# A graph-attention layer on one core: attention scores in two groups of three units over three banks, with other engine orders and the last two batches written out

## What is computed

```
h = relu(layernorm(x))                       # x: (32, 256, 384)
q, k, v = h @ Wq + bq, h @ Wk + bk, h @ Wv + bv
scores = einsum('bhqd,bhkd->bhqk', q, k) / 8
probs  = softmax(scores + where(adj, 0, -9e15))   # adj: (32, 256, 256)
ctx    = einsum('bhqk,bhkd->bhqd', probs, v)
out    = x + ctx @ Wf + bf
```

## Time and profile before

| what | value |
|---|---|
| time, median of 3 runs | 593.15 us (592.7 to 593.23) |
| the profiled execution, its own time | 594.17 us |
| its span, first to last instruction | 592.4 us |
| PE, PEld busy | 575.3 us, 429.6 us |
| ACT, POOL, DVE busy | 516.3 us, 491.4 us, 473.5 us |
| mean granted PE clock | 0.994 of full speed |

### The profile page before, as it was taken

One profiled execution on the slowest core, in us unless ns is written; L12 is line 12 of the kernel. 1 busy time (PEld: TensorE's weight loads), 2 busy tenths in 40 slices (PEclk: granted clock), 3 DMA queues, 4 the chain that ended last, 5 costly groups with the idle time before them and its releaser, 6 DMA issues.

```text
span 592.4 us, 17738 instructions
## 1 busy us (share of the span) xinstructions
PE 575.3 (97%) x6640; PEld 429.6 (73%) x6640; DVE 473.5 (80%) x1484; ACT 516.3 (87%) x1161; POOL 491.4 (83%) x533
## 2 busy tenths in 40 slices
PE   7997999999999999999999999999999999999986
PEld 7676777777777777777777777776777777777754
DVE  5988888888878878888887888888787778878664
ACT  2788999899999999999999999998999999999972
POOL 2779998888899888889988888988888898888870
PEclk9999999999999999999999999999999999999999
DMA  8048889879788989879897977789897787978662
GB/s 273 8 77 148 134 169 177 170 159 168 165 148 157 185 157 178 167 141 168 160 184 157 181 163 150 159 158 177 165 178 166 157 151 161 179 132 153 125 133 73
DMA packets 275640, 92.01 MB, mean 155 GB/s; under 512 B 257633, under 2 KB 275554, under 8 KB 275554
## 3 DMA queue, kind: packets, MB, share of 16 engines
q1 hardware_dynamic: 274352, 90.87, 79.8%
q10 hardware_dynamic: 1202, 0.01, 0.1%
HBM read 17.05 MB, written 12.58 MB: 50 GB/s over the span
## 4 chain that ended last, share of the span: by engine, by line
PE 82%; DVE 6%; ACT 5%; DMA 3%; issue 2%; POOL 1%; ACTq 0%; SPq 0%; DVEq 0%; POOLq 0%
PE ring L1043 18%; PE ring L1045 18%; PE ring L1044 18%; PE scores L1106 11%; PE ctx L1129 5%; PE ring L1141 3%; PE ctx L1131 3%; PE ctx L1130 3%; DMA p_cols<-p_rows 2%; DVE logits L750 2%; ACT probs L550 2%; DVE h_rows L767 1%; DMA bf_row<-in_L_gnn_bf_dram 1%; ACT qk L575 1%; PE ring L1171 1%
## 5 line engine op out<-in xcount | busy, mean ns | idle before, releaser
L428 POOL TENSOR_TENSOR p_rows<-probs,p_rows 128x512 f16<-128x512 f32 x190 | 220.6, 1161 | 32.2 <-ACT p_rows L555 31.8
L750 DVE CUSTOM_DVE_ANT_0 logits<-scores,mask,logit_unscale 128x256 f32<-128x256 f32 x384 | 169.0, 478 | 61.6 <-PE scores L1106 61.4
L550 ACT ACTIVATE probs<-logits,raised 128x256 f32<-128x256 f32 x372 | 168.9, 501 | 6.0
L1043 PE MATMUL ring<-h_cols,w_hi 128*128 128x256 f16 x576 | 157.2, 273 | 0.0
L1045 PE MATMUL ring<-h_cols,w_lo 128*128 128x256 f16 x576 | 157.0, 273 | 0.0
L1044 PE MATMUL ring<-h_cols,w_hi 128*128 128x256 f16 x576 | 156.9, 272 | 0.0
L414 POOL TENSOR_TENSOR split<-qk,split 128x512 f16<-128x512 f32 x96 | 111.5, 1161 | 36.4 <-DVE split L774 36.4
L555 ACT ACTIVATE p_rows<-probs 128x512 f16<-128x512 f32 x190 | 119.7, 630 | 6.0
L575 ACT ACTIVATE qk<-ring,qk_bias_s,qkv_ratio 128x256 f32<-128x256 f32 x192 | 96.5, 552 | 3.7 <-PE ring L1045 3.7
L1129 PEld LDWEIGHTS ctx<-v_hi,p_cols 128*128 128x128 f16 x756 | 68.9, 97 | 33.2 <-issue 27.7
L1129 PE MATMUL ctx<-v_hi,p_cols 128*128 128x65 f16 x756 | 88.2, 195 | 4.1 <-DMA p_cols<-p_rows 2.0
(11 more groups left out here) (116 smaller groups left out, 1158.6 us busy)
## 6 DMA issues: line engine op xcount, KB each, us to landing
x_in<-in_x_dram SPq DMA_DIRECT2D x32, 384.0 KB, 3.9
out_dram<-result SPq DMA_DIRECT2D x62, 192.0 KB, 2.2
p_cols<-p_rows SPq DMA_TRANSPOSE x190, 3.2
adj_in<-in_adj_dram SPq DMA_DIRECT2D x32, 64.0 KB, 2.9
w_raw<-in_L_gnn_Wq_dram SPq DMA_DIRECT2D x1, 576.0 KB, 5.6
w_raw<-in_L_gnn_Wv_dram SPq DMA_DIRECT2D x1, 576.0 KB, 8.0
w_raw<-in_L_gnn_Wf_dram SPq DMA_DIRECT2D x1, 576.0 KB, 9.0
h_cols<-h_rows SPq DMA_TRANSPOSE x29, 4.7
```

Of the source, the lines that this page charges most:

```text
L428: pool.tensor_tensor(p_rows[u][:, 1], probs[u % 3][:], p_rows[u][:, 0], ALU.subtract).then_inc(p_lo_ready, 1)
L550: act.activation(probs[u % 3][:, a], logits[u % 3][:, a], ACT.Exp, bias=raised[u % 3][:, a:a + 1], scale=-1.0).then_inc(probs_ready, 1)
L750: dve.tensor_tensor_reduce(out=logits[u % 3][:, a], in0=score_bank[a][:, u % 2 * S:(u % 2 + 1) * S], in1=mask[b.parity][:, t], scale=logit ...
L1043: pe.matmul(out_ap, a_hi, m_hi, start=first, stop=False)
```

## The change

It has four parts.

- **Three banks, groups of three.** The bank that held the start's peaks becomes a third score bank. `scores(b, units)` takes any units, and in a cycle it is called with units 0 to 2 and 3 to 5, 18 matmuls each. `score_of` places the six blocks. A block of unit 0's head 0 and one of unit 2's head 1 share a bank, and so PE waits, before the first matmul of the latter, for the last of the former (`shared_bank_done`).
- **Other orders in a cycle**, on DVE, POOL, ACT and SP.
- **The last two batches** (`PREV`, batch 30, and `LAST`, batch 31) are written out on each engine instead of the last call of `cycle` and the end; `cycle` runs for b = 1 to 29. A few buffers change banks there.
- **The start**: batch 0 is scored as (0, 1), (2), (3), (4, 5).

```diff
@@ constants and banks @@
-    GROUPS = UNITS // 2
+    GROUPS = UNITS // C
-        score_bank = [bank("scores0"), bank("scores1")]
-        peak_bank = bank("peaks")
+        score_bank = [bank(f"scores{n}") for n in range(3)]
+        peak_bank = score_bank[2]
+        def score_of(u, a):
+            n, column = ((1, 0), (2, 0), (0, 0), (2, S), (0, S), (1, S))[u % C * 2 + a]
+            return score_bank[n][:, column:column + S]
-            for k in range(1, B - 1):
+            for k in range(1, B - 2):
@@ scores on PE @@
-            def scores(b, g):
-                for u in (2 * g, 2 * g + 1):
+            def scores(b, units):
+                for u in units:
                     if u < C:
                         wait(pe, qk_hi_ready, b.count(C, u + 1))
                         wait(pe, qk_lo_ready, b.count(C, u + 1))
-                wait(pe, logits_ready, b.count(2 * UNITS, 4 * g))
-                for u in (2 * g, 2 * g + 1):
+                wait(pe, logits_ready, b.count(2 * UNITS, 2 * units[0]))
+                for u in units:
                     t, tile = u // C, split[b.parity][u % C]
                     for n, (q, k) in enumerate(((1, 2), (1, 3), (0, 2))):
                         for a in range(2):
+                            if u % C == 2 and n == 0 and a == 1:
+                                wait(pe, shared_bank_done, b.count(GROUPS, u // C + 1))
                             own = slice(D * a, D * a + D)
-                            mm = pe.matmul(score_bank[a][:, u % 2 * S:(u % 2 + 1) * S],
-                                           tile[own, q, t * P:(t + 1) * P], tile[own, k],
+                            mm = pe.matmul(score_of(u, a), tile[own, q, t * P:(t + 1) * P], tile[own, k],
                                            start=(n == 0), stop=(n == 2))
+                            if u % C == 0 and n == 2 and a == 0:
+                                mm.then_inc(shared_bank_done, 1)
                 mm.then_inc(scores_ready, 1)
@@ PE, cycle @@
-                    if here and u % 2 == 0:
-                        scores(b, u // 2)
+                    if here and u % C == 0:
+                        scores(b, range(u, u + C))
@@ POOL, cycle: the third split ahead of add_bias @@
                 if here:
                     probs_lo(b, 3)
                 if front:
+                    split_lo(b + 1, 2)
+                if here:
+                    probs_lo(b, 4)
+                if front:
                     add_bias(b + 1)
-                if here:
-                    probs_lo(b, 4)
-                if front:
-                    split_lo(b + 1, 2)
@@ DVE, cycle: unit 2 read ahead of v_lo; rows split behind unit 3; third cast behind the moments @@
                 if here:
+                    mask_and_max(b, 2)
                     v_lo_part(b, 0)
                     v_lo_part(b, 1)
-                if here:
-                    mask_and_max(b, 2)
+                if (b + 3).exists():
+                    layer_stats(b + 3, (0,))
                 if front:
                     qk_hi_part(b + 1, 0)
                 if before:
                     context_lo(b + -1, 0)
-                if (b + 2).exists():
-                    h_lo_rows(b + 2)
                 if here:
                     mask_and_max(b, 3)
                 if before:
                     divide(b + -1, 1)
+                if (b + 2).exists():
+                    h_lo_rows(b + 2)
                 if front:
                     qk_hi_part(b + 1, 1)
...
                 if here:
                     mask_and_max(b, 4)
-                if front:
-                    qk_hi_part(b + 1, 2)
                 if (b + 3).exists():
                     layer_stats(b + 3, (1,))
                     layer_moments(b + 3)
+                if front:
+                    qk_hi_part(b + 1, 2)
@@ PE, the end, up to the last probabilities @@
-            scores(LAST, 0)
+            scores(PREV, (0, 1, 2))
+            apply_probs(PREV + -1, 2)
+            project_qk(LAST, 0)
+            project_out(PREV + -2, 1)
+            scores(PREV, (3, 4, 5))
+            apply_probs(PREV + -1, 3)
+            transpose_context(PREV + -1, 0)
+            project_qk(LAST, 1)
+            apply_probs(PREV + -1, 4)
+            apply_probs(PREV + -1, 5)
+            project_qk(LAST, 2)
+            project_v(LAST, 0, (0,))
+            transpose_context(PREV + -1, 1)
+            project_v(LAST, 0, (1, 2))
+            project_out(PREV + -1, 0)
+            apply_probs(PREV, 0)
+            scores(LAST, (0, 1, 2))
+            project_v(LAST, 1)
+            apply_probs(PREV, 1)
             apply_probs(PREV, 2)
             project_out(PREV + -1, 1)
+            scores(LAST, (3, 4, 5))
             apply_probs(PREV, 3)
-            scores(LAST, 1)
             transpose_context(PREV, 0)
             apply_probs(PREV, 4)
-            scores(LAST, 2)
+            project_out(PREV, 0)
             apply_probs(PREV, 5)
-            project_out(PREV, 0)
```

More of the change, by code:

```diff
@@ L261, in pair, with scored @@
             return slice(j * P, (j + 1) * P)
+        def scored(b, u):
+            if b.k == 0:
+                return (1, 1, 2, 3, 4, 4)[u]
+            return 4 + (b.k - 1) * GROUPS + u // C + 1
         def w_scale(n):
@@ L517, in cycle @@
                 if front:
-                    split_lo(b + 1, 2)
+                    add_bias(b + 1)
             cycles(cycle)
@@ L524, in raise_last @@
                 pool.wait_ge(logits_ready, LAST.count(2 * UNITS, 2 * u + 2))
-                pool.tensor_scalar(raised[u % 3][:], least[u % 3][:], P_RAISE, None, ALU.add).then_inc(raised_ready, 1)
+                pool.tensor_scalar(raised[u % 3][:], least[u % 3][:], P_RAISE, None, ALU.add)\
+                    .then_inc(raised_last_ready, 1)
+            probs_lo(PREV + -1, 5)
+            add_bias(LAST)
+            split_lo(LAST, 0)
+            probs_lo(PREV, 0)
+            probs_lo(PREV, 1)
+            probs_lo(PREV, 2)
+            make_mask(LAST)
+            split_lo(LAST, 1)
+            split_lo(LAST, 2)
+            probs_lo(PREV, 3)
+            probs_lo(PREV, 4)
+            raise_last(0)
             probs_lo(PREV, 5)
-            raise_last(0)
             raise_last(1)
@@ L707, in context_hi_last @@
                 act.activation(ct_hi[1][:, chunks].rearrange("p c q -> p (c q)"),
-                               R_CT[1][:, chunks.start * P:chunks.stop * P], ACT.Copy).then_inc(ct_hi_ready, 1)
+                               ct_of(LAST, 1)[:, chunks.start * P:chunks.stop * P], ACT.Copy).then_inc(ct_hi_ready, 1)
+            v_hi_part(PREV, 1)
+            exps(PREV, 0)
+            qk_full(LAST, 0)
+            probs_hi(PREV, 0)
+            exps(PREV, 1)
+            exps(PREV, 2)
+            probs_hi(PREV, 1)
+            context_hi(PREV + -1, 0)
+            qk_full(LAST, 1)
+            probs_hi(PREV, 2)
+            exps(PREV, 3)
+            probs_hi(PREV, 3)
+            qk_full(LAST, 2)
+            exps(PREV, 4)
+            probs_hi(PREV, 4)
+            exps(PREV, 5)
+            v_hi_part(LAST, 0)
+            context_hi(PREV + -1, 1)
+            probs_hi(PREV, 5)
             exps_last(0)
+            v_hi_part(LAST, 1)
             probs_hi(LAST, 0)
-            v_hi_part(LAST, 1)
             exps_last(1)
@@ L715, in _ @@
             exps_last(2)
+            context_hi(PREV, 0)
             probs_hi(LAST, 2)
-            context_hi(PREV, 0)
             exps_last(3)
@@ L721, in _ @@
             exps_last(5)
+            context_hi(PREV, 1)
             turned_hi(4, 1)
-            context_hi(PREV, 1)
             turned_hi(5, 2)
@@ L742, in mask_and_max @@
                 t, j = u // C, u % C
-                wait(dve, scores_ready, b.count(GROUPS, u // 2 + 1))
+                wait(dve, scores_ready, scored(b, u))
                 if u == 0:
@@ L1010, in finish_last @@
                                          op1=ALU.add).then_inc(result_ready, 1)
+            mask_and_max(PREV, 0)
+            divide(PREV + -1, 0)
+            mask_and_max(PREV, 1)
+            mask_and_max(PREV, 2)
+            qk_hi_part(LAST, 0)
+            finish(PREV + -2, 1)
+            v_lo_part(PREV, 0)
+            mask_and_max(PREV, 3)
+            mask_and_max(PREV, 4)
+            v_lo_part(PREV, 1)
+            context_lo(PREV + -1, 0)
+            mask_and_max(PREV, 5)
+            divide(PREV + -1, 1)
+            qk_hi_part(LAST, 1)
+            qk_hi_part(LAST, 2)
+            finish(PREV + -1, 0)
             mask_and_max(LAST, 0)
+            v_lo_part(LAST, 0)
+            context_lo(PREV + -1, 1)
             mask_and_max(LAST, 1)
+            mask_and_max(LAST, 2)
             divide(PREV, 0)
             finish(PREV + -1, 1)
-            v_lo_part(LAST, 0)
             v_lo_part(LAST, 1)
-            mask_and_max(LAST, 2)
             mask_and_max(LAST, 3)
@@ L1024, in _ @@
             finish(PREV, 0)
+            context_lo(PREV, 1)
```

(15 more changed lines are left out.)

81 lines of the change are left out of this document (50 added, 31 removed).

## The result

The changed kernel takes **594.26 us** (median of 12 runs, 592.97 to 596.52), the kernel before, on the same chip, 593.1 (median of 12). The ratio is 1.0023, with a 95% interval of 1.0012 to 1.0033: **slower by 0.2%** where 584.9 us, 1.4% faster, was forecast, and outside the range of 581.5 to 590.5. The profiled execution has a span of 594.7 us against 592.4. It took 596.52 us and was the slowest of its twelve, so the profile overstates the loss: 2.3 us of span, where the medians differ by 1.2.

A forecast was written before the change was run, and what follows sets the result against it. PE was taken to bound the cycles; -5.9 + 1.1 + 0 - 3.5 = -8.3 us took the median from 593.15 to 584.9 us. Its own range was 582 to 587.5, with rivals A and B 581.5 to 590.5.

The forecast's parts named there:

- Fewer groups: PE in the 28 cycles for batches 2 to 29: one group edge pair less each, 0.21 us apiece, -5.9 us.
- The 0.32: Alternative cost in us of a score group's two edges on PE if each were a full drain; not used in the sum.
- The wait inside a group: PE's wait before the 14th of 18 score matmuls, already satisfied: 0.02 us each, +1.1 us, bounds 0 and +11.8.
- Lateness for DVE: A group's last matmul comes 0.33 us later for DVE; `divide` keeps its 0.12 us of slack, so no cost.
- `split_2` earlier: POOL's split, now needed by the next batch's first scores, is done some 0.4 us before PE comes: no cost.
- the 36.4 / 96: Step in the `split_2` sum: 0.38 us, on the mean, until POOL starts the split.
- The other moves: Unit 2 ahead of `v_lo`, rows split later: half a microsecond to three of slack against PE's need, costed at nothing.
- Rival A: Steady gain eaten by mid-group waits or a late `split_2`; only the end gains: about 590 us, chance 0.13.
- The start: Batch 0 has one group more, cycle 1 saves a group and a wait: sum 0, bounds -1 and +1 us.
- The end: From batch 30's first scores to the last `finish`: less idle and slow-clock PE time, -3.5 us, bounds -4.9 and 0.

The follow-up runs named there:

- e12: e2 with unit 5 scored by itself behind `apply_probs(b, 1)`, so three groups a cycle again with the same matmuls: 589.67 us.
- e11: e2 with five waits instead of one inside each group of scores, all satisfied when PE comes to them: 585.61 us.
- e2: Changed kernel with SP's load of x moved from ahead of unit 1's transposing DMA to behind unit 3's: 585.55 us.
- e4: Changed kernel with POOL's old order: additions of the output bias ahead of `probs_lo(b, 4)`, `split_2` behind it: 655.27 us.
- e10: Changed kernel with the load of x behind the transfer of unit 5 of the batch before, where SP then issues nothing: 584.06 us.
- e8: Kernel before the change with the load of x moved behind the transposing DMA of unit 2: 592.08 us.
- e9: Kernel before the change with SP waiting for the previous batch's first `context_lo` ahead of the load of x and unit 1's transfer: 593.3 us.
- e13: Changed kernel with SP's old order of two transfers, the rows of h ahead of unit 2: 591.62 us.
- e1: Changed kernel with POOL's two output-bias additions moved from behind `probs_lo(b, 4)` to between `probs_lo(b, 2)` and `split_1`: 607.29 us.
- e5: Changed kernel with the load of x moved behind the transposing DMA of unit 2: 590.89 us.
- e14: Kernel before the change, made late on SP as in e9, with unit 2's transfer ahead of the rows of h: 594.19 us.
- e7: Kernel before the change with one more, unused addition of 128 x 384 on POOL right ahead of `probs_lo(b, 1)`: 633.2 us.
- e15: Changed kernel with 64 more matmuls of 8 columns in the start, read by nobody, meant to shift PE's instruction packets: 615.5 us.

## Why the prediction was wrong

**Fewer groups, -5.9: right.** 0.21 a pair was forecast, 0.22 measured (e12). The 0.32 that I had worked out from the Trainium skill's full drain ("TensorEngine Tiling (Array Packing)", Key Properties) is too much here. The undisturbed period fell by 0.24, which is 6.8 us over 28 cycles.

**The wait inside a group, +1.1: nothing.** 1.09 us from scores to `apply_probs`, and four waits more changed nothing (e11).

**Lateness for DVE, nothing: right for `divide`, not for the casts.** No row shows PE waiting for `divide` in the cycles. But the 0.33 us by which a group is longer also delay `project_qk(b+1, 0)` (its last matmul starts 5.16 us behind the first scores in e2, 4.83 before) and the first cast (7.29, before 6.96), and from there pass down to POOL's splits.

**`split_2` earlier, hidden by 0.4 us: right, with 0.3 to 0.5 more to spare.** In the changed kernel it is done 0.9 us ahead of the scores on the median, in e2, with few waits, 0.7. One step of the sum was misread: the 36.4 / 96 is how long POOL had been idle before a split, not how long it took to start behind a cast, and the split of the earlier trace rows had no idle time at all. e4 shows that the new POOL order was needed.

**"The other moves ... are costed at nothing": this is the step that failed.** It looked at what each moved step feeds on PE and not at what is queued behind it, and it does not list the move of `add_bias` at all. What the runs show in its place is a lateness of 1.2 us in POOL's chain, in a schedule whose tightest transfer had 1.4 us to spare. The size is seen best in e2, which has the changed kernel's orders on POOL and DVE and few waits: `probs_lo(b, 1)` ends 8.87 us behind the first scores, against 7.67 before. Of these 1.2 us, 0.5 is POOL's new wait for the third cast, which `add_bias`, now behind it, no longer covers. Another 0.64 is that the second split starts later (4.66 us ahead of the next scores instead of 5.30): 0.33 for the longer group, 0.24 since the next scores come that much sooner, and some 0.1 on DVE. SP's issue and the landing come later with it, while PE's need, 14.00 us behind the scores before, is at 13.79. The prediction never set a landing time against PE's need. Before, unit 1 had a median slack (from landing to PE's first matmul on it) of 1.4 us; after, it had 0.4, and its landings scatter from 3.8 to 6.7. The price is 10.6 us in the profiled run. Rival A had the kind (a gain eaten by another wait), but not the place, and about half the price.

How far is this shown? Moving the load alone, with POOL untouched, gives 8.7 us back (e2) and 10.2 in the best place (e10); so the waits for the transfer are the loss. Before, with a median slack of 1.4 us, the same load cost 0.9 us (e8): the change made the schedule sensitive to it. Lateness alone isn't enough (e9). The new neighbour on SP has a share of about 3 us in the cycles (28 x 0.11, e13). Lateness alone in the changed kernel could not be taken away: the place tried for the additions collides with DVE (e1). There, issued at 8.17, unit 1 was tight in 7 cycles instead of 13, but with a longer period.

An estimate divides the loss. It crosses every issue with every landing time of batches 2 to 28 and adds up what comes later than 13.74 us behind the first scores, the changed kernel's need. Its issues with the landing times of before give 4.2 us, the issues of before with its landing times 5.3, both its own 9.9 (11.9 as they came in the run). By this estimate, then, lateness alone and slower landings alone would each make about half of it; with the landing times of e9 in place of before's, lateness alone makes 1.9. Why the landings are slower, apart from the neighbour's share, stays open.

**The start, 0: it was +1.6 in the profiled run.** PE waited 2.13 us at 51.77 (before 1.76 at 51.40), and from 53.19 its granted clock was 1.2 GHz instead of 2.4 for 3.41 us, which is worth 1.7 us. The window after, and the same of e13, where the clock stayed up and the first scores of batch 2 came 2.3 us earlier (last numbers: clock, DMA share, GB/s):

```profile
50.00:57.00 7.00, 5.23 (x49) 3.82 (x51) 2.62 (x4) 5.51 (x12) 7.00 (x8) 0.76 0.60 94
```

```profile
50.00:57.00 7.00, 5.89 (x79) 5.03 (x79) 4.08 (x11) 5.87 (x15) 6.95 (x7) 1.00 0.52 108
```

e5 waited 1.92 there and lost the clock, e10 waited 1.89 and kept it. Of the twelve timed runs of the changed kernel, seven have a mean granted clock of 1.0 and so no such stretch; their median is 593.89 us. That of the five with 0.994, as in the profiled run, is 595.64. At the full clock the start is like that of before (62.9 us in e13; 62.2 to 63.6 in the runs with before's orders in it, before, e8, e9 and e14).

**The end, -3.5: it was -3.0, right.** The last `finish` starts at 591.77, 37.3 us behind the first scores of batch 30 at 554.44, against 40.35. Idle PE in it is 3.2 us instead of under 3 (at 570.16, there for `POOL split`, 578.17, 582.61, 584.04 and 587.92), and the clock stays up:

```profile
575.00:580.00 5.00, 4.19 (x67) 3.18 (x66) 4.58 (x16) 4.68 (x10) 3.94 (x7) 1.00 1.13 165
```

With the load moved (e10), the median is 8.9 us below before, where 8.3 was forecast. The terms that I priced were sound in sum; what I took for zero ate them.

## What to carry to other kernels

An operation whose result is wanted late may still be filling a wait. Before you move it, follow what is queued behind it on its engine, through the queue's issue, to the landing, and compare the slack with the slowest landings, not with the usual one. Here the big load had a victim in three of the four other places tried (units 4, 3 and 3), and in the fourth one cycle of 27 was still long: put it where the transfers around it have the most slack, and look at every unit's slack again afterwards. Idle time of POOL beside `h_lo_rows`, a DVE operation on SBUF operands, was not free room. And before an inserted stretch of code counts as a test of chance, compare in time what it was to shift.

## What the hardware showed that I had not expected

- A transposing transfer of 128 x 1024 values of float16 lands 3.05 us after its issue if nothing is in its way, 4.2 with a load of 384 KB issued ahead of it, and with a 16 KB packet of instructions beside it up to 1.6 us later still. In the cycle shown, traffic stood near zero for 1.4 us from 0.6 us behind the packet's start.
- `h_lo_rows` on DVE takes 1.2 us with POOL idle beside most of it, 2.5 us with POOL's additions beside it (e1) and 3.0 in e7.
- 64 float32 matmuls of 8 columns, 128 in the profile, took 23.8 us in e15. The clock explains most of it: up to 11.94 us they start 0.109 us apart, as those of 128 columns just before them do (0.112), so fewer columns saved nothing; then the granted clock is 1.2 GHz for 23.9 us, though PE is never idle, and they start 0.213 apart.

```profile
12.00:31.80 19.80, 19.80 (x95) 19.80 (x95) 0.00 (x0) 0.00 (x0) 0.00 (x0) 0.50 0.16 52
```
